# Where nine small layer-norm steps of the next stage stand on VectorE among the last encoder jobs

## The reference

```python
b, s = x.shape                                   # 8 sequences of 256 tokens, D = 256
h = emb[x] + _pos_encoding(s, D)
for l in range(L):                               # 4 layers
    y = _layer_norm(h, ln_a[l, 0], ln_b[l, 0])
    ...                                          # 16 heads of 16: q, k, v, softmax, o
    h = h + o @ attn_w[l, 3] + attn_b[l, 3]
    y = _layer_norm(h, ln_a[l, 1], ln_b[l, 1])
    h = h + jax.nn.relu(y @ w1[l] + b1[l]) @ w2[l] + b2[l]
h = _layer_norm(h, norm_a, norm_b)               # a*(x-mean)/(sqrt(var)+eps)+b
h = h + attention2(_layernorm(h))                # rmsnorm, then qkv, windows of 128
h = h + experts(_layernorm(h))
```

## Time and profile before

| what | us |
|---|---|
| median of 3 runs | 2016.61 |
| lowest and highest | 2016.5 and 2016.9 |
| the profiled execution's own time | 2017.28 |
| its span | 2015.5 |
| PE busy | 1992.8 (99%) |
| DVE busy | 1297.4 (64%) |
| ACT busy | 1034.2 (51%) |
| POOL busy | 216.2 (11%) |

### The profile page before, as it was taken

The page is one execution under the profiler, slowest core; times in us unless marked ns, Lnnn a source line. Parts: engine busy times, 40 slices in busy tenths (PEclk is TensorE's granted clock), DMA queues, the critical chain, the costliest instruction groups (busy, mean ns, idle before and its releaser), DMA issues. The chain is left out here.

```text
span 2015.5 us, 42310 instructions
## 1 busy us (share of the span) xinstructions
PE 1992.8 (99%) x16486; PEld 1662.6 (82%) x16486; DVE 1297.4 (64%) x3340; ACT 1034.2 (51%) x3520; POOL 216.2 (11%) x257
## 2 busy tenths in 40 slices
PE   8999999999999999999999999999999999999999
PEld 5888888888888888888888887788888888877776
DVE  6767767767767767767768764767776646323232
ACT  5665666666666666666665662555455521111111
POOL 1101000000000000000000000000000000334444
PEclk9999999999999999999999999999999999999999
DMA  3100000200000400000000001300000100035542
GB/s 94 57 32 12 1 2 2 72 2 2 1 2 2 163 2 2 1 2 2 1 1 2 2 2 40 150 1 1 1 1 1 64 1 16 27 93 158 169 136 67
DMA packets 27203, 69.84 MB, mean 35 GB/s; under 512 B 9920, under 2 KB 17825, under 8 KB 23680
## 3 DMA queue, kind: packets, MB, share of 16 engines
q1 hardware_dynamic: 18432, 59.42, 8.7%
q0 software_dynamic: 6400, 5.63, 1.1%
q10 hardware_dynamic: 2176, 2.10, 0.3%
HBM read 61.16 MB, written 17.40 MB: 39 GB/s over the span
## 5 line engine op out<-in xcount | busy, mean ns | idle before, releaser
L595 ACT ACTIVATE probs<-bank,nmax 128x256 f32<-128x256 f32 x1024 | 471.2, 480 | 233.6 <-DVE nmax L796 233.1
L796 DVE TENSOR_REDUCE nmax<-bank 128x2 f32<-128x512 f32 x512 | 321.9, 681 | 48.8 <-PE bank L421 48.7
L434 PE MATMUL bank<-ident,probs 128*128 128x128 f32 x2048 | 272.9, 276 | 1.7 <-DVE pts L804 1.1
L434 PEld LDWEIGHTS bank<-ident,probs 128*128 128x128 f32 x2048 | 229.2, 140 | 50.0 <-issue 33.7
L466 PE MATMUL bank<-yT,weights 128*128 128x256 f32 x1024 | 236.7, 379 | 0.0
L604 ACT ACTIVATE pts<-bank 128x512 f32<-128x512 f32 x256 | 157.0, 613 | 153.7 <-PE bank L434 152.6
L478 PE MATMUL bank<-weights,aT 128*128 128x256 f32 x1024 | 231.7, 379 | 2.2 <-ACT probs L595 1.9
L595 ACT ACTIVATION_READ_ACCUMULATOR probs<-bank,nmax 128x1 f32 x1024 | 216.6, 212 | 0.0
L478 PEld LDWEIGHTS bank<-weights,aT 128*128 128x128 f32 x1024 | 191.9, 190 | 28.0 <-issue 2.8
L804 DVE COPY pts<-bank 128x512 f32<-128x512 f32 x256 | 175.5, 685 | 46.6 <-PE bank L434 42.3
L466 PEld LDWEIGHTS bank<-yT,weights 128*128 128x128 f32 x1024 | 187.3, 190 | 21.6
(11 more groups left out here) (233 smaller groups left out, 2970.6 us busy)
## 6 DMA issues: line engine op xcount, KB each, us to landing
wqkv<-in_experts SPq DMA_DIRECT2D x16, 1024.0 KB, 5.1
weights<-in_wtok SPq DMA_DIRECT2D x4, 2048.0 KB, 10.4
wqkv<-in_experts SPq DMA_DIRECT2D x16, 512.0 KB, 3.7
expert_rows<-xT_all SPq DMA_DIRECT2D x10, 546.0 KB, 16.6
xrows<-expert_rows SPq DMA_DIRECT2D x16, 273.0 KB, 3.2
weights<-in_wtok SPq DMA_DIRECT2D x3, 1024.0 KB, 4.7
wqkv<-in_wqkv SPq DMA_DIRECT2D x1, 3072.0 KB, 17.6
weights<-in_shared SPq DMA_DIRECT2D x1, 3072.0 KB, 12.5
```

The costliest lines, as they stand in the source:

```text
L434: last = pe.transpose(g[:, (NT * x + kb) * P:(NT * x + kb + 1) * P], p[:, x, kb * P:(kb + 1) * P], ident[:])
L595: last = nc.scalar.activation(probs[u % 8][:, x, :], g[:, x * S:(x + 1) * S], ACT.Exp, bias=nmax[j % 2][:, col:col + 1], accum_out=rsum[j ...
L796: nc.vector.tensor_reduce(nmax[j % 2][:, col:col + 2], g[:].rearrange("p (x s) -> p x s", x=2), AX.X, ALU.max, negate=True).then_inc(s_max, 1)
```

## The change

The same nine steps run, with the same instructions. Before, they stood in nine slots in a row, from (28, 0) to (30, 0). Now they stand only in slots 1 and 3, from (26, 3) to (30, 3):

| step | A0 | A1 | A2 | A3 | A4 | B0 | B1 | B2 | B3 |
|---|---|---|---|---|---|---|---|---|---|
| before | 28,0 | 28,1 | 28,2 | 28,3 | 29,0 | 29,1 | 29,2 | 29,3 | 30,0 |
| now | 26,3 | 27,1 | 27,3 | 28,1 | 28,3 | 29,1 | 29,3 | 30,1 | 30,3 |

On POOL the four `norm.root` calls move to fit. The work on PE, ACT and SP, and its order, is as before.

```diff
@@ -325,16 +325,16 @@
                 if j + 2 < B:
                     gather(range((j + 2) * NT, (j + 3) * NT))
                     positions(j + 2)
-                if j == JOBS - 4:
+                if j == JOBS - 5:
                     norm.root(nc, pool, expo, 0, 0)
-                if j == JOBS - 2:
-                    norm.root(nc, pool, expo, 1, 1)
                 if real(j - 1):
                     root(2, j - 1)
                 if j == JOBS - 4:
                     norm.root(nc, pool, expo, 0, 1)
                 if j == JOBS - 3:
                     norm.root(nc, pool, expo, 1, 0)
+                if j == JOBS - 2:
+                    norm.root(nc, pool, expo, 1, 1)
@@ -916,10 +916,13 @@
                         relu(j - 1, 3)
-                    if 0 <= GROUPS * (j - JOBS + 4) + c < 5:
-                        second_norm(0, GROUPS * (j - JOBS + 4) + c)
-                    if 0 <= GROUPS * (j - JOBS + 3) + c - 1 < 4:
-                        second_norm(1, GROUPS * (j - JOBS + 3) + c - 1)
+
+                    if c % 2:
+                        n = 2 * (j - JOBS + 6) + c // 2 - 1
+                        if 0 <= n < 5:
+                            second_norm(0, n)
+                        if 5 <= n < 9:
+                            second_norm(1, n - 5)
```

## The result

The changed kernel takes 2021.69 us (median of 12 runs, 2021.12 to 2022.38), the kernel before 2016.94 us beside it (median of 12). The ratio is 1.0023, with a 95% interval of 1.0015 to 1.003: slower by 4.75 us, where 4.72 were forecast. One of the twelve executions of the kernel before took 2293.82 us; without it the median is 2016.90. The profiled execution took 2022.24 us, with a span of 2020.4.

A forecast was written before the change was run, and what follows sets the result against it. PE was taken to bound the kernel, busy 1992.8 of 2015.5 us. New odd-slot losses of 8.95 us less 4.23 lost before gave 4.72 us more, taking the median from 2016.61 to 2021.3 us; range 2019.7 to 2022.4.

The forecast's parts named there:

- What bounds the kernel: PE, busy 1992.8 of 2015.5 us; a moved DVE step matters only where PE stands still for it.
- Free even tails, priced odd tails: Steps ending slots 1 and 3 cost PE time, 4.23 us for four before; those ending slots 0 and 2 nothing.
- Length less slack: An odd-slot step costs its DVE length less 0.06 us (slot 1) or 0.16 us (slot 3); nine total 8.95 us.
- The prices add: DVE waits 1.40 or 1.48 us before each odd tail, absorbing earlier lag, so the nine prices sum.
- Roots and the end of the chain at 0: Four moved POOL roots, and sequence 0's `w_yn` and B3's result written earlier or later, cost 0.
- rival 1: Idle time is the right reading, or short steps have more slack: +3.3 to +4.0 us, about 2020.3; chance 0.13.
- rival 2: Lags pile up between adjacent slots, so spreading steps recovers at best all 4.23 us: 2012.4 us; chance 0.04.
- rival 3: In slot (30, 1), POOL's root and B2 hold each other up: +5.4 us, 2022.0; chance 0.08, shared with no-slack sum.
- The threshold: Measurement can tell about 0.2%, 4.0 us, from no change; chances given: slower 0.76, "same" 0.20, faster 0.04.

The follow-up runs named there:

- the row of the other parity: Kernel before with the nine steps still in adjacent slots, shifted one slot to (27, 3) through (29, 3): 2017.64 us, ratio 1.0004.
- the additions in ordinary jobs: Kernel before plus one VectorE 128x512 addition ending one slot of jobs 4 to 23; slots 0 to 3: 2016.86, 2027.34, 2016.88, 2025.95 us.
- the halves: Kernel before with only sequence 0's steps moved as in the change: 2019.61 us, ratio 1.0012; with only sequence 1's: 2019.25 us, 1.0011.
- the additions behind slot 3: Kernel before plus one VectorE 128x512 addition at the end of slot 3 of jobs 4 to 23: 2025.95 us, ratio 1.0043.

## Why the prediction was right

**What bounds the kernel.** Right. Every microsecond of the change lies in slots of PE that lengthened behind a moved step.

**Free even tails, priced odd tails.** Right, shown by all nine steps on even slots (3.95 us less than before, 4.23 forecast), by the row of the other parity, and by the additions in ordinary jobs.

**Length less slack.** Right within 0.05 us for each of the nine. The largest miss is B2 (1.32 for 1.27); A3 (1.32 for 1.30) and B1 (0.89 for 0.87) come next. The slack of 0.16 us in slot 3 held: 0.14 to 0.17 in the run after. That of 0.06 in slot 1 was read from steps of about 1 us and is smaller for the long ones: with their lengths in the run after, 1.35 and 1.34 us, 0.03 is left for A3 and 0.02 for B2. Why is open.

**The prices add.** Right. In the run after too, each odd tail begins from a wait of VectorE, 1.40 to 1.41 us in slot 1 and 1.47 to 1.48 in slot 3, which wipes out the lag of the one before; the halves sum to the whole.

**Roots and the end of the chain at 0.** Right in sum: with the roots moved again and all steps on even slots, every slot from (27, 0) to (31, 0) had its yardstick length. The order of the roots was not tried by itself. By the order of the calls, either order as a whole, with the other's steps, would leave VectorE and GpSimd waiting for each other; the last root alone could have been moved, and that was not run.

**Starts or idle time (rival 1).** The starts were the right reading. By idle time the change would have been 3.7 us (7.1 against 3.4, and the new waits are 3.7 + 3.4 = 7.1 indeed), while the slots lost 4.82. The medians alone do not tell the two apart, since 3.0 to 6.1 us holds both; the additions behind slot 3 do, 4.2 us by idle time and 9.1 by the medians. What the prediction quotes from the Trainium skill (Trainium Kernel Development and Optimization, Performance Expectations) is said there of how close a kernel is to its roofline. That it also picks the reading of a stall was my inference, and it rests on these runs.

**Relief of neighbours (rival 2)** fell with the shifted row. **The root beside B2 (rival 3)** did meet the step, but the time fell on GpSimd, 1.11 us instead of 0.69. A longer instruction of GpSimd, an addition of 128x512, did hold VectorE up, by 0.95 us; none stands near the nine steps. Nothing waited for this root: the root was done at 1161.87, and VectorE wanted it only after two more row maxima.

**The threshold.** The forecast lay only 0.7 us above the 4.0 us that a measurement here can tell; the interval, 1.0015 to 1.003, lies above 1, but its lower end is below 0.2%. With a forecast that close, the share that I gave to "same" was needed.

## What to carry to other kernels

When an engine that does not bind gets extra work, ask what it does *next*, and who waits for that: here the same instructions were free at the end of one slot and cost 75 to 99% of their length at the end of the next. Find a stretch without them as a yardstick, compare start to start, and read off both the price and the slack. Spreading work out is worth nothing by itself; on even slots the sparse layout gained 4.0 us, on odd ones it lost 4.75. "Free" has an end, too: behind slot 0 it was at some 2.8 us.

## What the runs showed of the hardware

A GpSimd root over 128x2 numbers takes 0.69 us, but 1.04 to 1.11 us when a VectorE multiplication or addition of two SBUF inputs has begun 0.14 to 0.17 us before it. In the other order, with the root 0.14 to 0.15 us ahead, twenty such additions took 673 to 676 ns and were not held up.

A GpSimd addition of 128x512 with two SBUF inputs takes 1.26 to 1.27 us, but 1.45 and 1.52 us when it began during such a VectorE addition. The next VectorE addition began 0.35 and 0.42 us behind it and took 1.64 us instead of 0.69, to 0.54 us after GpSimd's end both times.

The Trainium skill (SBUF — State Buffer, Who interferes with whom) says that such a pair shares a port pair and that whichever starts first blocks the other for its whole length. That VectorE, when first, delays GpSimd agrees with the 1.04 to 1.11 us and the 1.45 and 1.52 us. That GpSimd, when first, blocks VectorE to its end agrees with the two additions of 1.64 us. It does not show in the 673 to 676 ns beside the root; it may be that the root uses the port for only a part of its 0.69 us, which no run here separates.

PE's idle time understates a stall in these profiles: 0.79 us idle stood for 0.97 us lost behind A1 before the change, 0.25 us idle for 0.49 behind A4 after it. The two waits, in the timelines of PE of the kernel before and of the kernel after:

```profile
1080.84 0.63 PE L348 MATMUL bank<-ident,yn 128*128 128x128 f32 x4 [0.79 <-DVE yn L750]
```

```profile
1104.51 3.69 PE L478 MATMUL bank<-weights,aT 128*128 128x256 f32 x16 [0.25 <-ACT probs L595]
```
